# An attention and feed-forward tower on one core: three pairs in flight instead of two, and one bank shared by the block's other work

## The reference

```
h = gelu(x[1:] @ W1 + x[0] @ W2 + b)                    # tokens, one readout row added to all
q, k, v = layernorm(h) @ qkv_w.T                         # 16 heads of 64
a = softmax(q @ k.T / 8 + relative_bias) @ v             # 255 x 255 per head
h = h + a @ o_w.T
g, u = layernorm(h) @ gate.T / 127, ... @ up.T / 127     # 768 hidden
h = h + (silu(g) * u) @ down.T / 127
```

## Time and profile before

| | PE | PEld | DVE | ACT | POOL |
|---|---|---|---|---|---|
| busy, share of the span | 93% | 85% | 86% | 72% | 44% |

### The profile page before, as it was taken

One profiled execution on the slowest core, in us unless ns is written; L12 is line 12 of the kernel. 1 busy time (PEld: TensorE's weight loads), 2 busy tenths in 40 slices (PEclk: granted clock), 3 DMA queues, 4 the chain that ended last, 5 costly groups with the idle time before them and its releaser, 6 DMA issues.

```text
span 2020.9 us, 42647 instructions
## 1 busy us (share of the span) xinstructions
PE 1883.2 (93%) x15402; PEld 1713.2 (85%) x15402; DVE 1735.1 (86%) x5248; ACT 1464.1 (72%) x4034; POOL 883.4 (44%) x1103
## 2 busy tenths in 40 slices
PE   3699999999999999999999999999999999999995
PEld 1588888888888888888888888888888888888884
DVE  3488998888898889898889899888889888889884
ACT  5577777777777777777777777777777777777773
POOL 0254444444444444444444444444444444444441
PEclk9799999999999999999999999999999999999998
DMA  6000000000000000000000000000000000000000
GB/s 206 30 1 14 14 10 14 14 14 7 14 9 14 14 15 6 14 12 11 15 14 6 14 14 9 14 14 15 7 14 9 14 15 14 6 14 13 3 7 11
DMA packets 24887, 34.36 MB, mean 17 GB/s; under 512 B 2449, under 2 KB 17810, under 8 KB 24674
## 3 DMA queue, kind: packets, MB, share of 16 engines
q1 hardware_dynamic: 15202, 20.03, 3.4%
q10 hardware_dynamic: 8704, 8.36, 1.3%
q0 software_dynamic: 768, 3.21, 0.4%
HBM read 23.17 MB, written 8.42 MB: 16 GB/s over the span
## 4 chain that ended last, share of the span: by engine, by line
PE 57%; DVE 19%; ACT 18%; issue 3%; POOL 0%; DMA 0%; SPq 0%; POOLq 0%; DVEq 0%
PE ps L455 32%; PE ps L512 8%; PE ps L523 7%; PE ps L502 7%; ACT prob L695 6%; DVE prob L839 4%; PE ps L465 3%; DVE hT L882 2%; DVE pT L849 2%; DVE gate L873 2%; ACT L695 2%; ACT L671 2%; DVE heads L859 2%; ACT pT L702 2%; DVE gated L877 2%
## 5 line engine op out<-in xcount | busy, mean ns | idle before, releaser
L432 POOL TENSOR_TENSOR prob<-prob,inv 128x510 f32<-128x510 f32 x512 | 530.3, 1038 | 795.3 <-DVE inv L854 795.2
L695 ACT ACTIVATE prob<-prob,neg_top 128x255 f32<-128x255 f32 x1024 | 509.6, 502 | 55.7 <-DVE neg_top L839 55.2
L702 ACT ACTIVATE pT<-ps 128x512 fp32r<-128x512 f32 x512 | 277.9, 594 | 241.9 <-PE ps L512 241.9
L455 PE MATMUL ps<-xnT,wqk 128*128 128x256 f32 x3072 | 424.9, 287 | 1.4 <-DVE xnT L814 1.4
L455 PEld LDWEIGHTS ps<-xnT,wqk 128*128 128x128 f32 x3072 | 378.7, 189 | 2.5 <-DVE xnT L814 1.8
L839 DVE CUSTOM_DVE_ANT_0 prob<-ps,bias 128x255 f32<-128x255 f32 x1024 | 370.6, 418 | 9.9 <-PE ps L502 8.3
L849 DVE TENSOR_TENSOR pT<-ps,pT 128x512 fp32r<-128x512 f32 x512 | 328.5, 683 | 1.8 <-ACT pT L702 1.8
L512 PE MATMUL ps<-ident,prob 128*128 128x128 f32 x2048 | 280.4, 280 | 35.3 <-DVE heads L859 31.7
L523 PE MATMUL ps<-pT,v 128*128 128x256 f32 x2048 | 294.2, 286 | 0.3 <-DVE pT L849 0.3
L512 PEld LDWEIGHTS ps<-ident,prob 128*128 128x128 f32 x2048 | 219.8, 141 | 76.1 <-DVE heads L859 55.0
L523 PEld LDWEIGHTS ps<-pT,v 128*128 128x128 f32 x2048 | 270.7, 189 | 8.1 <-DVE pT L849 0.5
(11 more groups left out here) (89 smaller groups left out, 2632.5 us busy)
## 6 DMA issues: line engine op xcount, KB each, us to landing
xt<-x_cols SPq DMA_DIRECT2D x32, 256.0 KB, 2.6
r_rows<-readout_rows SPq DMA_DIRECT2D x32, 128.0 KB, 3.1
out<-h ACTq DMA_DIRECT2D x32, 128.0 KB
out<-h ACTq DMA_DIRECT2D x32, 127.0 KB
flipped<-bias_rows POOLq DMA_DIRECT2D x1, 3072.0 KB, 17.5
staged<-w_qk SPq DMA_DIRECT2D x8, 256.0 KB, 6.0
staged<-w_v SPq DMA_DIRECT2D x4, 256.0 KB, 8.1
staged<-w_o SPq DMA_DIRECT2D x4, 256.0 KB, 3.3
```

The source lines that it names most:

```text
L432: pool.tensor_tensor(pr, pr, by, ALU.mult).then_inc(prob_done, 1)
L455: mm = pe.matmul(dst, lhs(a, k), rhs(b, k), start=(start and n == 0), stop=(stop and n == last), skip_group_check=skip)
L695: ex = act.activation(pr, pr, ACT.Exp, bias=neg_top[:, g, hh, t:t + 1], scale=-1.0, accum_out=total[:, g, hh, t:t + 1])
L702: act.activation(pT[:, hh, 0].rearrange("p k q -> p (k q)"), ps[:, bank_t[hh], :], ACT.Copy).then_inc(pT_hi, 1)
```

## The change

One step is now numbered G = 8 i + g through the whole run, and the stages stand further apart:

- PE in a step: queries and keys of G+1, scores of G, early piece, values times probabilities of **G-2** (was g-1), projection of **G-3** (was g-2), transposes of G-1, late piece. Transposes write `bank_t`; values times probabilities write a bank of their own, `bank_a`.
- `values`, `tokens`, both norm transposes, `gate_up` and `down` all use one bank, `bank_f`; each waits until the one before has been read out. `down` of a batch is one burst of 24 matmuls, a batch later than its `gate_up`s, for which all six hidden tiles are kept (`hT`). In the last batch each `gate_up` has a bank of its own.
- The sum of a pair's halves: ACT copies the whole bank (128 x 512) to `moved` in one instruction, and DVE adds across the partition halves.
- One reciprocal per pair instead of two. The lo of a hidden tile is made by POOL (was DVE), the hi of the second norm by ACT (was DVE). Tokens are processed in place in a buffer of three.
- Stores are issued by SP behind a load, not by ACT.

```diff
-        bank_qk, bank_f, bank_o, bank_d = 4, 5, 6, 7
-        GU_EARLY, GU_LATE = {4: 1, 5: 2, 6: 4}, {3: 0, 5: 3, 6: 5}
-        GU_BANK = (bank_d, bank_f, bank_f, bank_s[1], bank_f, bank_s[1])
-        V_BANK = (bank_f, bank_d, bank_d, bank_s[1])
+        bank_qk, bank_a, bank_o, bank_f = 4, 5, 6, 7
+        V_EARLY, V_LATE = {0: 0, 3: 3}, {1: 1, 2: 2}
+        GU_EARLY, GU_LATE = {5: 1, 7: 4}, {4: 0, 5: 2, 6: 3, 7: 5}
...
 # PE, one step
+                    if pair(G + 1):
+                        pe.wait_ge(qk_lo, count(PAIRS, *pair(G)))
+                        queries_keys(*pair(G + 1))
+                    if pair(G):
+                        scores(i, g)          # waits for biased of G-1
+                    early()
+                    if pair(G - 2):
+                        if pair(G - 3):
+                            pe.wait_ge(o_added, count(PAIRS, *pair(G - 3)))
+                        values_probs(*pair(G - 2))
+                    if pair(G - 3):
...
+                        project(bb, gg)
+                    if pair(G - 1):
+                        probs_transposed(*pair(G - 1))
+                    late()
...
 # ACT, one step
+                        exps(*pair(G - 1), 1)
+                        tanh(*gu_at(G - 1, GU_LATE))
+                        values_hi(*v_at(G - 1, V_LATE))
+                        gelu(i + 1)                    # g == 1
+                        probs_hi(*pair(G - 2), 1)
+                        gated_hi(*gu_at(G - 1, GU_EARLY))
+                        queries_keys_hi(*pair(G + 1))
+                        gated_hi(*gu_at(G - 1, GU_LATE))
+                        values_hi(*v_at(G, V_EARLY)); norm_hi(1, i - 1)
+                        tanh(*gu_at(G, GU_EARLY)); norm_hi(0, i + 1)
+                        exps(i, g, 0)
+                        heads_moved(*pair(G - 2))
+                        probs_hi(*pair(G - 1), 0)
...
 # DVE, one step
+                        probs_lo(*pair(G - 2), 0)
+                        pre_gelu(i + 1)                # g == 1
+                        inverse(*pair(G - 1))
+                        layer_var(1, i - 1)            # g == 3
+                        gating(*gu_at(G - 1, GU_LATE))
+                        values_lo(*v_at(G - 1, V_LATE))
+                        probs_lo(*pair(G - 2), 1)
+                            queries_keys_lo(*pair(G + 1))   # g == 1: behind add_bias
+                            add_bias(i, g)
+                        output(i - 2)                  # g == 1
+                        residual(i - 1)                # g == 2
...
+                        gating(*gu_at(G, GU_EARLY))
+                        heads_added(*pair(G - 2))
+                        layer_sums(1, i - 1, ...)      # g == 2
...
 # POOL, one step
+                        normalise_probs(*pair(G - 1))
+                        gated_lo(*gu_at(G - 1, GU_EARLY)); gated_lo(*gu_at(G - 1, GU_LATE))
+                        heads_split(*pair(G - 2))
...
 # PE, other work
+                        if g == 1 and i >= 2:
+                            pe.wait_ge(pre_done, ...); down(i - 2, has_lo)
+                        if g == 5 and prev:
+                            pe.wait_ge(gated_done, count(MT, i - 1, 0)); gate_up(i - 1, 1, has_lo)
...
 # the sum of a pair's halves
-                    act.activation(moved[0:DH, :], ps[DH:P, bank_t[0], 0:T], ACT.Copy)
-                    act.activation(moved[DH:P, :], ps[0:DH, bank_t[1], 0:T], ACT.Copy)
+                    act.activation(moved[:], ps[:, bank_a, :], ACT.Copy).then_inc(o_moved, 1)
-                    dve.tensor_tensor(heads[0:DH, :], ps[0:DH, bank_t[0], 0:T], moved[0:DH, :], ALU.add)
-                    dve.tensor_tensor(heads[DH:P, :], ps[DH:P, bank_t[1], 0:T], moved[DH:P, :], ALU.add)
+                    dve.tensor_tensor(heads[0:DH, :], ps[0:DH, bank_a, 0:T], moved[DH:P, 0:T], ALU.add)
+                    dve.tensor_tensor(heads[DH:P, :], ps[DH:P, bank_a, T:2 * T], moved[0:DH, T:2 * T], ALU.add)
...
 # SP
+                for i in range(B + 1):
+                    if i + 1 < B:
+                        sp.wait_ge(pre_done, count(1, i))
+                        if i >= 2:
+                            sp.wait_ge(h1_done, count(1, i - 2))
+                        load(i + 1)
+                    if i >= 2:
+                        store(i - 2)          # waits for out_done
+                store(B - 1)
```

More of the change, by code:

```diff
@@ L372, in tower_kernel, with token_tile, pair, v_at @@
         out_done = sem("out_done")
[L374 to L385, removed]
+        def token_tile(batch):
+            return xt[:, batch % 3].rearrange("p k n -> p (k n)").rearrange("p (t n) -> p t n", t=TT)
+        def pair(G):
+            return divmod(G, PAIRS) if 0 <= G < B * PAIRS else None
+        def v_at(G, table):
+            i, g = divmod(G, PAIRS)
+            return (i, table[g]) if 0 <= i < B and g in table else None
+        def gu_at(G, table):
+            i, g = divmod(G, PAIRS)
+            return (i - 1, table[g]) if 1 <= i < B and g in table else None
+        def tanh_tile(batch, m):
+            return moved[:, 0:T] if batch == B - 1 and m % 2 else tanh_g[:]
+        def gu_bank(batch, m):
+            return m if batch == B - 1 else bank_f
+        def run(step):
+            for G in range(B * PAIRS + 4):
+                i, g = divmod(G, PAIRS)
+                step(G, i, g, 1 <= i < B, i < B - 1)
         with nc.Block() as block:
@@ L418, in layer_norm @@
                                        ).then_inc(ln_rstd[n], 1)
-                layer_norm(0, 0)
[L422 to L443, removed]
@@ L445, in _, with normalise_probs, heads_split @@
-                run(iteration)
+                def normalise_probs(batch, g):
+                    pool.wait_ge(inv_done, count(PAIRS, batch, g))
+                    for hh in range(2):
+                        pr = prob[:, g % 2, hh, :, 0:S]
+                        by = inv[:, g % 2, hh].rearrange("p (t a) -> p t a", a=1).broadcast_to([P, TT, S])
+                        pool.tensor_tensor(pr, pr, by, ALU.mult).then_inc(prob_done, 1)
+                def heads_split(batch, g):
+                    pool.wait_ge(o_added, count(PAIRS, batch, g))
+                    pool.sem_inc(passed, 1)
+                    pool.tensor_copy(oT[:, g % 2, 0, :], heads[:]).then_inc(o_hi, 1)
+                    pool.wait_ge(o_hi, count(PAIRS, batch, g))
+                    pool.tensor_tensor(oT[:, g % 2, 1, :], heads[:],
+                                       oT[:, g % 2, 0, :].bitcast(F32), ALU.subtract).then_inc(o_lo, 1)
@@ L447, in _ @@
+                run(step)
+                for m in range(MT):
+                    gated_lo(B - 1, m)
             @block.tensor
@@ L458, in split_mm, with tokens @@
                     return mm
[L460 to L468, removed]
+                def tokens(batch):
+                    pe.wait_ge(x_in, count(32, batch, 31))
+                    for t in range(TT):
+                        for k in range(KD):
+                            mm = pe.matmul(ps[:, bank_f, t * D:(t + 1) * D], xt[:, batch % 3, k, t * P:(t + 1) * P],
+                                           w1[:, k, :], start=(k == 0), stop=(k == KD - 1))
+                    mm.then_inc(tok_mm, 1)
                 def norm_transposed(n, batch):
@@ L516, in values_probs @@
                 def values_probs(batch, g):
+                    if g % 4 == 0:
+                        pe.wait_ge(v_lo, count(4, batch, g // 4 * 2 + 1))
                     for hh in range(2):
@@ new lines, in step, with finish @@
+                    if pair(G - 3):
+                        bb, gg = pair(G - 3)
+                        if gg == 0 and bb > 0:
+                            pe.wait_ge(h1_done, count(1, bb - 1))
+                        project(bb, gg)
+                    if pair(G - 1):
+                        probs_transposed(*pair(G - 1))
+                    late()
+                def finish(has_lo):
+                    pe.wait_ge(out_done, count(1, B - 2))
+                    norm_transposed(1, B - 1)
+                    for m in range(MT):
+                        gate_up(B - 1, m, has_lo)
+                    down(B - 1, has_lo)
@@ L770, in _ @@
+                gelu(0)
                 norm_hi(0, 0)
                 queries_keys_hi(0, 0)
-                run(iteration)
+                run(step)
+                norm_hi(1, B - 1)
+                tanh(B - 1, 0)
+                for m in range(MT):
+                    if m + 1 < MT:
+                        tanh(B - 1, m + 1)
+                    gated_hi(B - 1, m)
             @block.vector
@@ L944, in _ @@
                 pre_gelu(0)
-                layer_norm(0, 0, h0[:, 0], gelu_done)
-                normalise(0, 0, h0[:, 0])
+                layer_sums(0, 0, token_tile(0), gelu_done)
+                layer_var(0, 0)
+                normalise(0, 0, token_tile(0))
                 norm_lo(0, 0)
                 queries_keys_lo(0, 0)
```

(5 more changed lines are left out.)

447 lines of the change are left out of this document (200 added, 247 removed).

## The result

| | time, median of 4 | range | to before, 95% interval |
|---|---|---|---|
| before | 2022.09 us | | |
| after | 1951.22 us | 1948.79 to 1952.05 | 0.9644 [0.9628, 0.9661] |

The kernel is 3.6% faster. 1926 was forecast, with 1905 to 1948 as the likeliest case's own range and 1903 to 1982 as the whole. The mechanism came as forecast. The size was 25 us too good. The profiled execution took 1951.19 us, its span 1949.3.

What follows compares the result with a forecast made beforehand. PE was taken to bound the kernel; start 71.9, batches 50.5 + 54.1 + 1655.9 (29 x 57.1) + 53.6 and end 38.1 gave 1924.1, plus 1.8: 1926 us. Likeliest case 1905 to 1948; 8 in 10, 1903 to 1982.

Steps and rivals of the forecast that it cites:

- The waits that go: PE's transposes behind heads_added, down behind a hidden tile's lo, norm transposes behind normalise: 1.92 us a batch, to be removed.
- The products: PE's matmul bursts: 55.96 us a batch, unchanged by the new order; with 0.6 of gaps a floor of 56.6.
- six of the seven bursts: Argument for gaps of only 0.6 us a batch: these bursts follow each other at the spacing of their matmuls.
- values 3: PE's fourth burst of values, in g3, behind the read-out of values 2: a margin of 0.2 us, so no wait.
- Cost 0: The store between output (g1) and residual (g2), about 7 us of room: free, at worst 1 us per batch.
- `gate_up` 1: PE's burst behind the gating of tile 0: late by 0.36 us, making the batch 57.0.
- five of my margins: Margins of PE's waits in the walk put at 0.0 to 0.3 us, cited in favour of "Half of it".
- Half of it: Rival, 20%: bank_f, read by ACT and DVE in turn, comes late at several bursts; 1.8 us a batch, 1982.
- Slower: Rival, 8%: the ring becomes the bound through costlier handovers; at 0.21 more each, 61.7 us a batch, 2069.
- the ring: Work that ACT and DVE hand to each other in every step: 53.3 us a batch, 93% of PE's.
- Less: Rival, 5%: the gaps of 0.6 and the lateness of 0.36 do not come; 56.0 us a batch, 1892.
- no change: Rival, 3%: the same loss returns elsewhere; 59.97 us a batch with only the end shorter, 2016 to 2026.

Runs made afterwards that it cites:

- experiment 4: Changed kernel with values times probabilities back in the transposes' banks, transposes waiting until heads are added: 2380.42 us (two runs), 1.1773 to the kernel before.
- experiment 2: Changed kernel with the eps addition of the second norm moved ahead of the reciprocal in DVE's step: 1926.43 us, 0.9527 to the kernel before.
- experiment 1: Changed kernel with the batch's output written to and stored from normed, so residual waits for no store: 1938.64 us, 0.9588 to the kernel before.
- Experiment 5: Changed kernel with two copies of 64x256 to moved instead of one of 128x512: 1974.92 us, 0.9768 to the kernel before.
- experiment 7: experiment 3's kernel with the copy to moved made twice, the second waiting for the first: 1982.37 us, 0.9801 to the kernel before.
- experiment 6: Changed kernel with the lo of the hidden tiles made by DVE again, except the last batch's six: 1966.57 us, 0.9723 to the kernel before.
- experiment 8: experiment 3's kernel with the second half of each store issued by ACT instead of SP: 1919.55 us, 0.9495 to the kernel before.
- experiment 3: Changed kernel with the edits of experiment 1 and experiment 2 together: 1917.55 us, 0.9486 to the kernel before.

## Why the prediction was nearly right, and where it was off

**The waits that go.** Right. All three of the earlier trace rows went, and experiment 4 shows that in the new order the first would be back without the own bank. But the prediction read only half of the second. It took "up to 897" in the earlier trace rows for a spread. In the trace of before 93 of the 192 subtractions take over 0.6 us; each of these 93 began while POOL was in its multiplication (L432), and none of the other 99 began beside a running instruction of POOL. The wait of `down` stood behind such a stretched one all 29 times:

```profile
949.32 1.04 POOL L432 TENSOR_TENSOR prob<-prob,inv 128x510 f32<-128x510 f32 x1 [2.86 <-DVE inv L854]
949.74 0.89 DVE L882 TENSOR_TENSOR hT<-gated,hT 128x256 fp32r<-128x256 f32 x1
...
950.69 0.75 PE L455 MATMUL ps<-wd,hT 128*128 128x256 f32 x4 [0.73 <-DVE hT L882]
```

So some 0.46 of that 0.73 was the collision which experiment 2 found in another instruction. Another order on DVE might have won it without a deeper pipeline; that was not tried.

**The products.** The floor was put at 56.6 (55.96 and 0.6 of gaps). Without any wait of PE it measures 56.87. Inside it two errors cancel in part. The transposes take 0.79 in the new order, not 0.85: 8 x 0.06 = 0.5 less. The gaps are 1.4, not 0.6. The largest part is `gate_up`: 1.02 to 1.04 (910.07 to 911.11 above) instead of 0.95, six times, together 0.46. It was priced by the form of its matmuls and not read; in the trace of before it already takes 1.03 ahead of scores (951.27 to 952.30). The rest: queries and keys 1.58 after transposes (1.68 after tokens) instead of 1.49, values times probabilities 1.06 after scores and 1.03 after norm transposes instead of 0.95, the halves of the tokens 0.77 instead of 0.68, `down` 2.94 instead of 2.85. The argument "six of the seven bursts" took its bursts from an order in which most of those neighbours did not occur. The sign "if the bursts' own spacing grows" thus came in part. (The eight steps as written add up to 56.7, not 56.6.)

**The step that failed: values 3, "0.2".** The walk had this margin right for the terms that it knew. Its two prices were missing. The store was "Cost 0", with "about 7 us" of room. The room is 7.4: in experiment 1, where nothing is waited for, `residual` starts 7.4 us after `output` ends. The store's way needs 7.8 (942.29 to 950.08). The bound of 8.1 us, 1 us per batch, had been named, and the measured cost is 0.27. The eps addition was counted at its 0.17 of before, and not as something that a neighbour on POOL can stretch: 0.80 at the margin, and the larger part of it. Together 0.93 a batch (57.80 - 56.87), 29 x 0.93 = 27 us.

**`gate_up` 1, "late by 0.36".** Not so: its slot is 0.94. The normalise ahead of that gating took 0.62 in the mean before. In the new place it takes 0.45:

```profile
L811 DVE TENSOR_SCALAR normed<-xt,mean_var,rstd 128x256 f32<-128x256 f32 x64 | 26.0, 450 | 1.9 <-POOL rstd L434 0.9
```

The place itself was right, though. Experiment 5 made it late by 0.45 with 0.17 us of more work, experiment 7 by 0.8. Of the "five of my margins" only four are 0.0 to 0.3; the fifth can only be this one, at -0.36.

**The other margins.** `gate_up` 2 and 3 (0.0 and 0.3) are real, as experiment 6 shows. Norm transposes (0.6) came without a wait.

**The engines.** DVE 49.5 against 47.8, of which 0.80 are the eps addition; the rest I did not follow up. ACT 43.6 against 44.1, POOL 30.9 against 31.9. POOL's subtraction takes what was assumed:

```profile
L454 POOL TENSOR_TENSOR hT<-gated,hT x192: 728/741/755, 159.9 to 1939.0; 128x256 fp32r<-128x256 f32 x192
```

The held addition of 0.08 a pair that the Trainium skill's rule (VectorE: DVE Perf Modes, "Two Vector instructions with no wait between them") would bring does not show in the durations. No run isolates it.

**The ends.** The first queries and keys began at 72.11, those of batch 2 at 176.44 (forecast 71.9 + 50.5 + 54.1 = 176.5). Batch 31 took 55.1 against 53.6, with the wait of values 3 again and 0.87 of `gate_up` 4. The end took 41.7 against 38.1:

```profile
1918.89 1.31 PE L484 MATMUL ps<-wo,oT 128*128 128x256 f32 x6 [2.24 <-POOL oT L449]
...
1923.52 0.69 DVE L869 TENSOR_TENSOR h<-ps,xt 128x512 f32<-128x512 f32 x1 [6.05 <-DMA out<-h]
...
1941.27 0.33 SPq L409 DMA_DIRECT2D out<-h  x1
```

The last projection is done at about 1920.2, and `residual` starts at 1923.52: it waits for the store of batch 30, whose `down` now comes a batch later and so just ahead of it. Without that wait, in experiment 1, the stretch from the last projection to the end is 2.4 us shorter, so it is the larger part of the 3.6. The same "cost 0" failed twice, in the steady part and at the end.

**The sum.** 29 x (57.80 - 57.1) = 20.3, batch 31 1.5, end 3.6: 25.4 of the 25.2 us by which the time is over 1926.

**The rivals.** "Half of it" named values 3 as late by 0.3, for lateness of ACT and DVE throughout. It was late by 0.90, at this place alone, for two reasons of its own. "Slower" did not come: experiment 7 put 4.8 us a batch on the ring, of the 6.7 which separate its 53.3 from 59.97, and still stayed 2% under the time of before. "Less" and "no change" did not come either.

**Left open.** What the deeper pipeline alone is worth, or `down` a batch later alone: neither was tried apart from the bank. Nor a store whose second half is cut otherwise. The ring was not pushed so far that it would bound.

## What to carry to other kernels

When a kernel is at 95% of its main engine, walk the new order burst by burst and list the margins. Then distrust every term in front of a margin under 0.3 us: price the DMA that a reused buffer waits for, each issue by itself, and look at what a neighbour on the other engine does just then. Work of an engine that is a quarter idle is not free where its margin is that small (0.17 us of a copy cost 0.66 a batch). And a signal that starts POOL is best given after the small DVE instruction beside it, not before.

## What the runs showed of the hardware that I had not expected

- A DVE instruction on 128x2 elements takes 0.97 us beside POOL's multiplication and 0.17 without it (experiment 2). In the kernel before, a subtraction of 128x256 took 0.89 beside it and 0.43 without.
- Of a store in rows of 1 KB, the half with 127 rows lands 7.3 us after its issue. The half with 128 rows is through in 1.4 (experiment 8). The load of 256 KB takes 2.7:

```profile
xt<-x_cols SPq DMA_DIRECT2D x32, 256.0 KB, 2.7
```

- Split over two queues the store is no shorter (experiment 8): 8.9 us from issue to the end of the span, against 8.0 for one queue (experiment 3).
- Additions whose two inputs lie in different halves of the partitions take the same 417 and 428 ns as those in the same half.
